# Latent attention on one core: scores of two pairs of key tiles ahead of the values of four, six score banks, and denominators inverted across partitions

## What is computed

```python
kv_rope = kv_c * cos[None] + _rotate_half(kv_c) * sin[None]
q_r = jnp.einsum('bshq,hqr->bhsr', q_big, W_qr)
k_r = jnp.einsum('bld,hdr->bhlr', kv_rope, W_kr)
scores = jnp.einsum('bhsr,bhlr->bhsl', q_r, k_r)
attn = jax.nn.softmax(scores, axis=-1)
ctx_c = jnp.einsum('bhsl,bld->bhsd', attn, kv_rope)
```

## Time and profile before

| what | value |
|---|---|
| median of three runs | 1906.14 us (1904.16 to 1909.09) |
| the profiled execution: its span, which the page gives as its time | 1905.6 us |
| PE (TensorE matmul) busy | 1505.3 us, 79% |
| DVE (VectorE) busy | 1418.2 us, 74% |
| ACT (ScalarE) busy | 1058.1 us, 56% |
| POOL (GpSimd) busy | 638.9 us, 34% |
| the latent loop in the trace | 371.1 to 1015.2 us |
| mean granted clock of TensorE | 0.855 |

### The profile page before, as it was taken

One profiled execution on the slowest core, in us unless ns is written; L12 is line 12 of the kernel. 1 busy time (PEld: TensorE's weight loads), 2 busy tenths in 40 slices (PEclk: granted clock), 3 DMA queues, 4 the chain that ended last, 5 costly groups with the idle time before them and its releaser, 6 DMA issues. The chain is left out here.

```text
span 1905.6 us, 37670 instructions
## 1 busy us (share of the span) xinstructions
PE 1505.3 (79%) x12653; PEld 910.4 (48%) x12668; DVE 1418.2 (74%) x2445; ACT 1058.1 (56%) x1759; POOL 638.9 (34%) x653
## 2 busy tenths in 40 slices
PE   1777776999999999999996746880687859956792
PEld 0455553433333333333334635870466537735682
DVE  6888865789898999989986774435688736667574
ACT  1777754766666666666663333440567535536461
POOL 1222211244545545455420234551233210026242
PEclk9665656999999999999997767995799879968897
DMA  6920000112111121111200144434000010023334
GB/s 163 333 87 1 1 1 33 28 36 50 39 40 48 35 51 37 43 46 35 53 11 2 32 121 134 133 110 133 1 2 0 0 25 1 0 86 125 103 107 155
DMA packets 79003, 116.28 MB, mean 61 GB/s; under 512 B 12530, under 2 KB 59834, under 8 KB 78484
## 3 DMA queue, kind: packets, MB, share of 16 engines
q1 hardware_dynamic: 69011, 91.53, 17.0%
q0 software_dynamic: 7776, 21.28, 3.2%
q10 hardware_dynamic: 2112, 2.10, 0.3%
HBM read 59.74 MB, written 40.19 MB: 52 GB/s over the span
## 5 line engine op out<-in xcount | busy, mean ns | idle before, releaser
L2603 DVE TENSOR_TENSOR lat_dsum<-lat_dsum,lat_Pb 125x896 f32<-125x896 f32 x320 | 414.8, 1296 | 62.2 <-ACT lat_Pb L2537 56.1
L2537 ACT ACTIVATE lat_Pb<-banks 125x896 f32<-125x896 f32 x384 | 331.4, 915 | 175.7 <-PE banks L2460 175.0
L2415 PE MATMUL banks<-lat_Pb,lat_kv 125*64 125x448 f32 x1536 | 332.5, 554 | 0.0
L2454 PE MATMUL banks<-lat_QH,lat_kT 128*125 128x448 f16 x768 | 184.5, 363 | 2.7 <-DVE lat_QT L2561 1.9
L2370 POOL TENSOR_TENSOR lat_kk<-lat_rot,lat_kk 125x768 f16<-125x768 f32 x32 | 71.6, 2237 | 317.5 <-ACT lat_kk L2509 317.5
L2415 PEld LDWEIGHTS banks<-lat_Pb,lat_kv 125*64 125x64 f32 x1536 | 93.4, 136 | 154.2 <-issue 153.0
L2454 PEld LDWEIGHTS banks<-lat_QH,lat_kT 128*125 128x125 f16 x768 | 89.7, 137 | 114.8 <-ACT lat_Pb L2537 89.1
L2917 POOL DMA_INDIRECT sent_outputs<-moe_yb,moe_yidx x98 | 99.0, 1010 | 135.4 <-ACT moe_yb L3174 108.4
L3055 PE MATMUL banks<-moe_w2d,moe_gT 88*128 (+3 forms) x780 | 103.9, 285 | 18.7 <-DVE moe_gT L3392 10.0
L2460 PE MATMUL banks<-lat_QL,lat_kT 64*125 64x448 f16 x768 | 114.2, 376 | 0.0
L3380 DVE COPY moe_xTb<-banks 128x1024 f16<-128x1024 f16 x49 | 33.7, 689 | 92.0 <-PE banks L3022 59.7
(11 more groups left out here) (440 smaller groups left out, 3291.2 us busy)
## 6 DMA issues: line engine op xcount, KB each, us to landing
moe_xb<-sent_rows SPq DMA_DIRECT2D x49, 257.0 KB
lat_raw<-in_ctx_dram SPq DMA_DIRECT2D x32, 375.0 KB
sent_rows<-zero SPq DMA_DIRECT2D x1, 7453.0 KB, 47.9
lat_QH<-lat_QT SPq DMA_DIRECT2D x64, 112.0 KB, 2.2
lat_QL<-lat_QT SPq DMA_DIRECT2D x64, 112.0 KB, 2.2
moe_arena<-sent_outputs SPq DMA_DIRECT2D x12, 512.0 KB, 6.5
sent_rows<-zero SPq DMA_DIRECT2D x1, 5140.0 KB, 64.4
sent_outputs<-zero SPq DMA_DIRECT2D x1, 4096.0 KB, 39.4
```

The costliest lines, as they stand in the source:

```text
L2415: ins = nc.tensor.matmul(ps[u * DC:(u + 1) * DC, 4 + par, 0:8 * T], kv[:, par, tt, :], Pb[:, tt % NPB, u, :], start=tt == 0, stop=tt == KT ...
L2454: nc.tensor.matmul(ps[0:KP, 2 * u + tt % 2, 0:8 * T], kT[:, par, tt, 0:KP], queries(QH, u), start=True, stop=False)
L2537: nc.scalar.activation(Pb[:, slot:slot + 2, u, :], ps[0:KP, 2 * u:2 * u + 2, 0:8 * T], ACT.Exp, scale=1.0 / QSCALE).then_inc(exp_done, 1)
L2603: ins = nc.vector.tensor_tensor(dsum[:, par], dsum[:, par], Pb[:, tt % NPB], ALU.add)
```

## The change: what it does

The key parts are laid out otherwise: a tile of `kk` holds the high parts of two neighbouring key tiles side by side, or their low parts. `scores` does for a pair and a half u six matmuls on 64 rows, the even tile on the upper rows and the odd tile on the lower, alternating. TensorE's body has three groups instead of six pairs: the scores of two pairs (four calls), then the values of the four tiles before them. The scores rotate over three double banks, 0 to 5; one value accumulator is left, bank 6, which VectorE copies to `pv` before the next batch's first values; bank 7 holds transposes and denominators in turn. The last four tiles of keys of a batch are turned within that batch.

ScalarE copies the denominators to `den`; SyncE spreads one row of each half over 64 partitions, 7 numbers on each (`den7`); VectorE inverts those 7 columns; SyncE writes them to DRAM and loads them back broadcast into `rD`. VectorE then multiplies `pv` by `rD`. The checks of size are made once after the loop. `Pb` has 8 tiles. `B16` is made by GpSimd ahead of its loop. The diff, cut to its core:

```diff
@@ -2272,29 +2272,40 @@
             QALL = 7 + NG * 16
 
             def halves(par, low):
-                units = kk[:, par].rearrange("p (a q) u d -> p a (q u) d", q=2)
-                return units[:, :, 1:3, :] if low else units[:, :, 0:4:3, :]
+                return kk[:, par, low:KT:2, :]
...
             def paired(a):
-                return a.rearrange("p (a q) d -> p a q d", q=2)
-
-            NPB = 6
+                return a.rearrange("p (a q) d -> p a (q d)", q=2)
+
+            NPB = 8
+
+            def tile_slot(tt, par):
+                return (tt + 4 * par) % NPB
...
+            kk = sb("kk", [KP, 2, KT, 2 * DC], F16, c=main)
-            rD = sb("rD", [P, 8 * T], c=main)
+            rD, pv = sb("rD", [P, 8 * T], c=main), sb("pv", [P, 8 * T], c=main)
...
                    def body(b, par):
+                        if not live(b, B):
+                            return
+                        if past(b, 1) and live(b + 1, B):
+
+                            sp.wait_ge(rotated, b)
+                            load_rows(b + 1, (par + 1) % 2)
                         if past(b, 2):
-
-                            sp.wait_ge(rotated, b - 1)
-                            load_rows(b, par)
                             sp.wait_ge(ql_made, QALL)
                             sp.wait_ge(s_done, (b - 1) * KT)
                         elif not past(b, 1):
...
+                        if past(b, 2):
+                            spread_reciprocals(b - 2)
+
+                    def spread_reciprocals(b):
+
+                        sp.wait_ge(den_kept, b + 1)
+                        for u in range(2):
+                            sp.dma_start(den7[u * DC:(u + 1) * DC, :],
+                                         den[u * DC:u * DC + 1, :].rearrange("o (p e) -> o p e", e=DR)
+                                         ).then_inc(den_in, 16)
+                        sp.wait_ge(rec_made, b + 1)
+                        sp.dma_start(recs.rearrange("u (p e) -> (u p) e", e=DR),
+                                     rec7[:, ds(b, 1), :].rearrange("p o e -> p (o e)")
+                                     ).then_inc(rec_sent, 16)
+                        sp.wait_ge(rec_sent, 16 * b + 16)
+                        if past(b, 1):
+                            sp.wait_ge(ct_made, b)
+                        for u in range(2):
+                            sp.dma_start(rD[u * DC:(u + 1) * DC, :],
+                                         recs[u:u + 1, :].broadcast_to([DC, 8 * T])
+                                         ).then_inc(rec_in, 16)
 
                     load_rows(0, 0)
                     load_rows(1, 1)
-                    over_tiles(sp, body, 0, n=B)
+                    over_tiles(sp, body, 1, n=B)
+                    spread_reciprocals(B - 2)
...
+                    nc.gpsimd.tensor_copy(B16[:, :, 0, :], Bs[:]).then_inc(bh_made, 1)
+                    pool.wait_ge(bh_made, 1)
+                    nc.gpsimd.tensor_tensor(B16[:, :, 1, :], Bs[:], B16[:, :, 0, :],
+                                            ALU.subtract).then_inc(bl_made, 1)
...
+                        elif past(b, 2):
+                            pe.wait_ge(den_kept, b - 1)
+                        bank = ps[:, 7, :].bitcast(F16)
...
+                        if tt == 0 and past(b, 1):
+
+                            pe.wait_ge(pv_kept, b)
...
                     def denominators(b, par):
+                        pe.wait_ge(kT_made, min(b + 1, B - 1) * NTURN + 2 if isinstance(b, int)
+                                   else b * NTURN + (NTURN + 2))
...
+                    def scores(b, par, pair, u):
+                        n = 2 * pair + u
+                        if past(b, 1) or n >= 3:
+
+                            pe.wait_ge(exp_done, b * KT + (n - 2))
+                        for m, (low, Q) in enumerate(((0, QH), (0, QL), (1, QH))):
+                            for q in range(2):
+                                rows = slice(q * DC, (q + 1) * DC)
+                                ins = nc.tensor.matmul(
+                                    ps[0:KP, n % 3 * 2 + q, 0:8 * T],
+                                    kT[rows, par, 2 * pair + low, 0:KP],
+                                    Q[rows, par, 8 * u:8 * u + 8, :].rearrange("p h t -> p (h t)"),
+                                    start=m == 0, stop=m == 2)
+                        ins.then_inc(s_done, 1)
...
+                        for g in range(3):
+                            if g == 0:
+                                pe.wait_ge(kT_made, b * NTURN + 1)
+                                pe.wait_ge(spread[par], 4 * half_count(b, par))
+                            if g == 2:
+                                pe.wait_ge(kT_made, b * NTURN + 2)
+                            for pair in (2 * g, 2 * g + 1):
+                                for u in range(2):
+                                    scores(b, par, pair, u)
+                            if g == 0:
+                                turn(b, par, 1)
+                            if g == 2 and live(b + 1, B):
+                                turn(b + 1, (par + 1) % 2, 0)
+                            for tt in range(4 * g - 4, 4 * g):
+                                if g:
                                     values(b, par, tt)
                                 elif past(b, 1):
                                     values(b - 1, (par + 1) % 2, KT + tt)
-                            if pair == 1 and past(b, 1):
+                            if g == 0 and past(b, 1):
                                 denominators(b - 1, (par + 1) % 2)
...
-                    values(B - 1, 1, KT - 2)
-                    values(B - 1, 1, KT - 1)
+                    for tt in range(KT - 4, KT):
+                        values(B - 1, 1, tt)
                     denominators(B - 1, 1)
...
+                    def keep_denominators(b):
+                        act.wait_ge(den_done, b + 1)
+                        if past(b, 1):
+                            act.wait_ge(den_in, 32 * b)
+                        nc.scalar.activation(den[:], ps[:, 7, 0:8 * T], ACT.Copy).then_inc(den_kept, 1)
...
+                        for n in range(KT):
+                            pair, u = n // 2, n % 2
+                            slot = tile_slot(2 * pair, par)
+                            act.wait_ge(s_done, b * KT + (n + 1))
...
+                            nc.scalar.activation(Pb[:, slot:slot + 2, u, :],
+                                                 ps[0:KP, n % 3 * 2:n % 3 * 2 + 2, 0:8 * T],
+                                                 ACT.Exp, scale=1.0 / QSCALE).then_inc(exp_done, 1)
+                            if n == 3:
+                                evacuate(b, par, 1)
+                                if live(b + 1, B):
                                     high(b + 1, (par + 1) % 2)
+                            if n == 7 and live(b + 1, B):
+                                rows(b + 1, (par + 1) % 2)
+                            if n == 4 and past(b, 1):
+                                keep_denominators(b - 1)
+                            if n == 10 and live(b + 1, B):
+                                evacuate(b + 1, (par + 1) % 2, 0)
...
+                    def reciprocals(b):
+                        dve.wait_ge(den_in, 32 * b + 32)
+                        nc.vector.reciprocal(rec7[:, ds(b, 1), :].rearrange("p o e -> p (o e)"),
+                                             den7[:]).then_inc(rec_made, 1)
+
+                    def keep_context(b):
+                        dve.wait_ge(pv_done, (b + 1) * KT)
+                        if past(b, 1):
+                            dve.wait_ge(ct_made, b)
+                        nc.vector.tensor_copy(pv[:], ps[:, 6, 0:8 * T]).then_inc(pv_kept, 1)
+
+                    def context(b, source):
+                        nc.vector.tensor_tensor(CT[:, ds(b, 1), :].rearrange("p o n -> p (o n)"),
+                                                source, rD[:], ALU.mult).then_inc(ct_made, 1)
...
+                            if tt == 2 and past(b, 1):
+                                keep_context(b - 1)
+                            if tt == 6 and past(b, 1):
+                                reciprocals(b - 1)
+                            if tt == KT - 2 and past(b, 1):
+                                dve.wait_ge(pv_kept, b)
+                                dve.wait_ge(rec_in, 32 * b)
+                                context(b - 1, pv[:])
```

More of the change, by code:

```diff
@@ L2439, in body @@
                             return
-                        def queries(Q, u, rows=slice(0, P)):
-                            return Q[rows, par, 8 * u:8 * u + 8, :].rearrange("p h t -> p (h t)")
-                        for pair in range(KT // 2):
-                            both = (2 * pair, 2 * pair + 1)
-                            for u in range(2):
-                                if pair == 0 and u == 0:
```

(46 more changed lines are left out.)

90 lines of the change are left out of this document (34 added, 56 removed).

## The result

The changed kernel took 1873.47 us, the median of four runs (1870.21 to 1876.76), against 1906.24 us of the kernel before beside it: a ratio of 0.983, 95% interval 0.981 to 0.985. The forecast was 1875.4 us. The profiled execution spans 1872.8 us.

The account below looks back on a forecast made before the run. TensorE's order of starts was taken to bound the kernel: 24.0 us off 30 batches (19.81 to 19.01 each), 0.5 off the first, 6.2 off the last, 30.7 off 1905.6, giving 1875.4 us; 8 in 10 range 1857 to 1900.

Parts of the forecast that it names:

- TensorE bounds, and its price is the change of shape: TensorE's latent loop: its order of starts sets the period; fewer matmul shape changes save 1.77 us a batch over three groups.
- Twos on 64 rows 0.19 apart: TensorE's scores: concurrent pairs of 64-row matmuls start every 0.19 us, bounds 0.19 and 0.24.
- rival 4: TensorE's scores: twos on 64 rows stay 0.24 apart, period 20.0, about 1904 us; chance 0.06 unchanged and 0.03 slower.
- Its last case: TensorE's scores: 64-row matmuls not concurrent at all, 0.19 for each of 24, 6 us a batch, 2080 us.
- The wait at the fourth unit: Each group's fourth scores call waits for the first's exponential to free its double bank: 0.23 us a group, 0.69 a batch.
- VectorE: VectorE's work a batch falls from 18.0 to about 15.1 us, losing the 2.94 us reciprocals and gaining copy, small reciprocal, product.
- cover of 2.6 to 4 us: Slack before TensorE waits: 2.6 us for VectorE's copy of value sums, 4 us for the chain of denominator transfers.
- rival 2: VectorE or ScalarE late in places, losing 0.5 us a batch, 15 us, time 1890; chance 0.17.
- Transfers: Denominators inverted through a chain of three DMA legs, each landing in 2.2 us, with 4 us of cover.
- rival 3: The chain of transfers sets the period; with legs of 5.4 us, period 22.0 and time 1965; chance 0.06.
- The first batch: Loop's first batch: loses two tiles of values but ScalarE then holds it; 0.5 us off, bounds 0 and 2.3.
- The last batch: Loop's last batch: its reciprocal starts at 22.4 us instead of 28.58, 6.2 us off.

## Why the prediction was right

- **TensorE bounds, and its price is the change of shape.** Right. The forecast period was 19.01 and the undisturbed batch takes 19.00; groups 6.87 against 6.89, 5.80 against 5.82 and 6.34 against 6.29. The TensorEngine Tiling page of the Trainium skill (Key Properties) has it that a change of tiling mode drains the engine; the rows here agree in that 0.09 us is paid on both sides of a transpose.
- **Twos on 64 rows 0.19 apart.** Right, rival 4 is out. (Its last case counts 24 twos where a batch has 36; the 6 us and the 2080 fit 36 x 0.19 = 6.84 above the forecast, 6.0 above the 19.81 of before.)
- **The wait at the fourth unit.** Right, 0.66 us a batch measured against 0.69; it is what three double banks for four units leave over. The sign for it came too: the loads at 607.92 had been idle for 0.43 us and were released by the exponential.
- **VectorE.** This term was mis-sized: 15.1 us a batch were forecast and it is 17.4. I took over the additions' mean of before and did not ask what stood beside GpSimd then: the reciprocal of 2.94 us, which reads PSUM, ran at full speed beside it. Two rows of the kernel before, from its timeline:

```profile
622.14 2.94 DVE L2576 RECIPROCAL lat_rD<-banks 128x448 f32<-128x448 f32 x1
...
623.16 1.81 POOL L2364 TENSOR_TENSOR lat_rot<-lat_rot 125x768 f32<-125x768 f32 x1
```

Taken from the two timelines over 30 batches, GpSimd's 9.6 us a batch overlapped the reciprocal by 2.7 and additions by 5.4 before; after, its 9.9 us overlap additions by 8.3. That this is why the mean rose is argued from these overlaps; that GpSimd's work makes additions long at all is shown by the run with less of it. So the cover of 2.6 to 4 us was used up in some batches. The mean batch lost 0.29 (19.29 less 19.00), 8.7 us over 30: rival 2, at about half its price, was part of the truth. Two of the prediction's own signs failed with this term: VectorE was to be below 80% busy and is at 90% (521.32 of 578.70), and TensorE was not to wait for `pv`, which it did in two batches for 2 us and in most of batches 2 to 8 for less.
- **Transfers.** They landed in 1.8, 1.4 and 2.8 us, near the 2.2 I took, and rival 3 did not come. The 2.0 us that the prediction cites for a DMA from the Trainium skill (DMA: Bandwidth & Descriptors, Anatomy of one DMA) is the page's fit for transfers that GpSimd issues; these SyncE issued, and the write to DRAM landed in 1.4. What was late in the chain was no transfer: the small reciprocal behind addition 6 was the late link. That it could be moved I did not see. The page of the kernel after has the broadcast with its KB and its median from issue to landing:

```profile
lat_rD<-lat_reciprocals SPq DMA_DIRECT2D x62, 112.0 KB, 2.8
```

And the waits of the kernel after between 400 and 940 us have the product behind it (us in all, times, longest):

```profile
DVE lat_QT L2623 <- DMA lat_rD<-lat_reciprocals: 17.1, 20, 1.3
```

So 2.8 us to land, and 17.1 us of waiting by VectorE in 20 of its products, where nothing was idle for the broadcast in the kernel with the earlier reciprocal.

- **The first batch** gained 4.95 and not 0.5: it held the lower clock for part of it before (0.84) and does not now (1.00). The clock is not all of it. The kernel before with B16 ahead has the old order of TensorE and half as long at the lower clock in its first batch, 373.0 to 376.4 where it was 372.9 to 379.7. Its first batch (PEclk 0.91):

```profile
370.63:390.55 19.92, 19.09 (x100) 7.23 (x100) 14.12 (x10) 14.39 (x17) 9.56 (x5) 0.91 0.01 3
```

That is 21.26 - 19.92 = 1.34 us less for half of it, so about 2.7 for the whole, an estimate. Some 2.3 us are then left for the order, the upper bound that I gave and not the 0.5 I took.
- **The last batch** gained 6.56 against 6.2.
- The sum came out 2 us off because the terms missed on both sides: 8.7 lost to stalls, 4.5 more from the first batch, and 5.8 from stretches that I don't credit to the change. The mechanism on TensorE was right; that the total came within two microseconds is luck.

Open: why exactly two batches of 30 stall by 2 to 4 us in each profile of the kernel after. Less work on GpSimd or an earlier reciprocal on VectorE ends them, but what sets the two engines in or out of step was not tried.

## What to carry to other kernels

Count the changes of matmul shape in TensorE's order, not only its columns: work that can be written in one shape saves them. Before calling an engine covered, see what its long instructions ran beside: with one gone that its neighbour did not slow, more of the neighbour's work can fall on those that it does slow. When an engine is nearly full, move its short links of a chain of transfers to the first place where their input is there: here one line took the ratio from 0.986 to 0.981, about a third of what the whole change had gained.

## What the runs showed of the hardware

- Two matmuls on 64 rows each, in different banks, start within 0.01 us of one another and every 0.19 us, as often as one on 128 rows; a change between 64 rows, 128 rows and 64 output partitions costs 0.09 to 0.10 us and 0.05 on the next first one, and a change into or out of transposes 0.09 (614.09 to 614.37, and 614.77 to 614.92).
- A VectorE addition of 896 float32 columns from two tiles in SBUF takes 1.09 us alone and 2.5 beside GpSimd; its copy out of PSUM took 0.61 at 933.44, in the middle of GpSimd's work. GpSimd's sum of the rotation took 1.81 us at 623.16 beside the reciprocal out of PSUM, and 2.54 at 612.04 beside additions.
- A reciprocal on VectorE takes 2.94 us for 448 columns and 0.19 for 7.
- TensorE was idle for 1.98 us up to 934.20, and its granted clock was 0.50 from 934.80 to 938.20; in batch 10 it was idle for 2.07 us, and the clock stayed at 1.00.
